# Folding the value norms into the output weights, and four buffers for the copied attention products

## Chip, cores and metric

The kernel runs on one core of one Trainium2 chip. The metric is the device time in microseconds (us) of one execution. One pair of numbers is kept apart throughout: the time of an execution, and the span, which is the stretch from the first to the last instruction that the profiler recorded in it.

## The reference

Four sequences of 512 tokens and width 512 go through one transformer layer: layer norm, attention, layer norm, residual; then layer norm, a gated feed-forward, layer norm, residual. The part that matters here:

```python
xq = rms_norm(x @ wq.T, q_norm_w)      # 32 query heads of 64
xk = rms_norm(x @ wk.T, k_norm_w)      # 8 key heads, each used by 4 query heads
xv = x @ wv.T                          # 8 value heads, each used by 4 query heads
scores = q @ k.T / 8 + alibi           # causal, window of 256 keys
out = softmax(scores) @ v
y = out.reshape(tokens, 2048) @ wo.T   # wo: 512 x 2048
```

Values are float32. The kernel gets float32 accuracy from TensorE by splitting every operand into a rounded part and a remainder (`_hi`, `_lo`) and adding three products.

## The kernel before

**Stage 1, projections.** For each sequence the queries, keys and values are computed and stored to DRAM. The value weights are first divided by a norm for each value column (`vn`, 512 numbers, one for each of 8 x 64 columns), so that values fit a pair of float16 numbers. The norms are computed once into a tile whose 128 partitions all hold the same 512 numbers, and stored to DRAM as `vn_scr` (128 x 512). So the attention's product has to be multiplied by `vn` again somewhere.

**Stage 2, attention and output projection.** Sixteen pairs of value heads are worked through, `for n in range(16)`: pair `n` holds value heads `2n` and `2n + 1` over all sequences (`s` = 0, 1 inside a pair), and for each of them four tiles of 128 queries (`i`), and for each of those four query heads: 32 units `u` in a pair. A unit is: scores (PE, L1322), bias and clamp (DVE `u_sb`, L1030), exponential (ACT `p_sb`, L781), transposes (PE, L1410), rounding and remainder (ACT `pT_hi`, DVE `pT_lo`), products with the values (PE, L1426 to L1428). Every engine runs a fixed order of work; a later step of a unit runs a few units behind the first. From pair 4 on PE also runs the output projection of one tile for each pair (L1449), four pairs behind; in pairs 0 to 3 there is none.

After each four units (one query tile of four heads, numbered `a` = 8n + 4s + i here) the product is finished:

- `take_values` (ACT, L901) copies 4 x 65 columns out of PSUM into `o_raw`; column 64 is the sum of the probabilities. There are two buffers, and the copy `a` waits until `o_mid` of `a - 2` is done.
- `invert_sums` (DVE, L1156) takes the reciprocals into `inv_sum`, also two buffers.
- `finish_o` (POOL) runs two operations: `o_mid = o_raw * inv_sum` (L672), then, after a wait for the first, `o_out = o_mid * v_norm` (L678).
- `store_o` (SP, L474) stores `o_out` to DRAM.

POOL's order in pair `n` is written out by hand:

```python
for i in range(2, 4): finish_o(n - 1, 1, i)
make_bias(n, 1)                 # needed by DVE's unit 16 of pair n
split_late(n, 0, 16)            # two late normalisations' remainders
for i in range(4):
    finish_o(n, 0, i)
    if tile < 0 and i in (2, 3): split_wo(n, i - 2)
make_bias(n + 1, 0)             # needed by DVE's unit 0 of pair n + 1
split_late(n, 16, 32)           # three of them
for i in range(2):
    finish_o(n, 1, i)
    if tile < 0: split_wo(n, 2 + i)
```

`tile = n - 4`, so `split_wo` runs in pairs 0 to 3 only: it makes `wo_hi` and `wo_lo` of one 128 x 512 chunk of the output weights (16 chunks, loaded four at a time by `load_wo` on SP). The late normalisations are those of the last sequence's queries and keys, which stage 1 leaves over: 17 of them in units 2, 4, 18, 20 and 22 of pairs 0 to 3 (five in each of pairs 0 to 2, two in pair 3); each is a DVE operation (`raw`, L1070), an ACT rounding (`qk`, L824), a POOL remainder (`qk`, L697) and a store on SP (L444). After the last one, in pair 3, SP waits until all stores of stage 1 have landed (`stage1_stored`), then stores `o_out`, and then loads keys and queries of pair 4 (`load_heads`, L457 and L458).

**Stage 3, the rest.** Four tiles of the output projection are left at 896 us, and then the feed-forward runs until the end.

Of the kernel before, what the change touches and what calls it, by code (L numbers as in the profile page):

```python
# [25 lines left out]
F32 = mybir.dt.float32  # L26
# [3 lines left out]
ALU = mybir.AluOpType  # L30

P = 128
B, T, D = 4, 512, 512
H, G, HD = 32, 8, 64
REP = H // G
# [3 lines left out]
TT = T // P  # L39
# [31 lines left out]
AHEAD = 2  # L71
TWINS = LAG * UNITS - 2 * TT
RING = 4
PIECE = 3
DMA = 16
RATIO = 2.0 ** (-8.0 / H)
# [2 lines left out]
O_COLS = HD + 1  # L79
# [103 lines left out]
def at_least(eng, sem, value):  # L183

    if isinstance(value, int) and value <= 0:
        return
    eng.wait_ge(sem, value)
# [18 lines left out]
def sandwich_layer(nc, x, wqT, wkT, wvT, woT, q_norm, k_norm, gateT, upT, downT, gate_s, up_s, down_s, out):  # L206
# [9 lines left out]
    vn_scr = nc.dram_tensor("vn_scr", [P, G * HD], F32, kind="Internal").ap()  # L216
    z_scr = nc.dram_tensor("z_scr", [B * TT, P, D], F32, kind="Internal").ap()

    with ExitStack() as ctx:
        def sb(scope, name, shape, dt=F32):  # L220
            return scope.enter_context(nc.sbuf_tensor(name, shape, dt))
# [4 lines left out]
        def sems(names):  # L226
            return [sem(name) for name in names.split()]
# [41 lines left out]
        with ExitStack() as s2:  # L269
            q_st = sb(s2, "q_st", [P, 2, REP, T], F32R)  # L270
            k_st = sb(s2, "k_st", [P, 2, 2, T], F32R)
            v_st = sb(s2, "v_st", [P, 2, TT, V_COLS], F16)
            bias1 = sb(s2, "bias1", [P, REP, WIN])
            y_raw = sb(s2, "y_raw", [P, D])
            sb(s2, "spare4", [P, REP * WIN - D])
            v_norm = sb(s2, "v_norm", [P, G + 2, HD])
            f_bits = sb(s2, "f_bits", [P, PARTS, D])
            used_bits = sb(s2, "used_bits", [P, D])
            u_sb = sb(s2, "u_sb", [P, RING, WIN])
            low = sb(s2, "low", [P, RING])  # L280
            p_sb = sb(s2, "p_sb", [P, RING, WIN])
            pT_hi = sb(s2, "pT_hi", [P, RING, WIN], F16)
            pT_lo = sb(s2, "pT_lo", [P, RING, WIN], F16)
            inv_sum = sb(s2, "inv_sum", [P, 2, REP])
            sb(s2, "spare", [P, REP * HD])
            o_raw = sb(s2, "o_raw", [P, 2, REP, O_COLS])
            o_mid = sb(s2, "o_mid", [P, REP, HD])
            o_out = sb(s2, "o_out", [P, TT, REP, HD])
            wo_stage = sb(s2, "wo_stage", [P, TT, D])
            wo_hi = sb(s2, "wo_hi", [P, QC, D], F32R)  # L290
            wo_lo = sb(s2, "wo_lo", [P, QC, D], F32R)
            o_in = sb(s2, "o_in", [P, 2, TT, 2 * REP * HD])
            oT_hi = sb(s2, "oT_hi", [P, 2, 4, P], F32R)
            oT_lo = sb(s2, "oT_lo", [P, 2, 4, P], F32R)
            x_res = sb(s2, "x_res", [P, D])
            y_n = sb(s2, "y_n", [P, D])
            z_out = sb(s2, "z_out", [P, D])
            sb(s2, "spare3", [P, S1_END - S2_END])
            bias = [sb(s2, "bias0", [P, REP, WIN]), bias1]
# [3 lines left out]
        with ExitStack() as s4:  # L303
# [41 lines left out]
        dist_ready, bias_ready, vn_loaded = sems("dist_ready bias_ready vn_loaded")  # L345
        s_psum, u_ready, p_ready, pT_psum, pT_hi_ready, pT_ready, pv_done = sems(
            "s_psum u_ready p_ready pT_psum pT_hi_ready pT_ready pv_done")
        inv_sum_ready, o_raw_ready, o_mid_ready, o_ready = sems(
            "inv_sum_ready o_raw_ready o_mid_ready o_ready")
        tile_loaded, tile_last = sems("tile_loaded0 tile_loaded1"), sems("tile_last0 tile_last1")  # L350
        wo_hi_ready, wo_ready, res1_loaded, oT_psum, oT_hi_ready, oT_ready, oT_used = sems(
            "wo_hi_ready wo_ready res1_loaded oT_psum oT_hi_ready oT_ready oT_used")
# [32 lines left out]
        def hold(eng):  # L385


            eng.sem_inc(held, 1)
# [3 lines left out]
        def _(sp):  # L392
# [155 lines left out]
                store_o(n, 1, 0)  # L548

            sp.wait_ge(gemm_done, NGEMM * B)  # L550
            sp.dma_start(v_norm[:, 0:G].rearrange("p g d -> p (g d)"), vn_scr).then_inc(vn_loaded, DMA)
            sp.dma_start(v_norm[:, G:G + 2].rearrange("p g d -> p (g d)"), vn_scr[:, 0:2 * HD]).then_inc(vn_loaded, DMA)
            for n in range(B * TT):
                attend(n)
            for i in range(1, TT):
# [65 lines left out]
        def _(pool):  # L621
# [45 lines left out]
            def finish_o(n, s, i):  # L667

                a = 2 * TT * n + TT * s + i
                pool.wait_ge(inv_sum_ready, a + 1)  # L670
                at_least(pool, o_ready, a)
                nc.gpsimd.tensor_tensor(out=o_mid[:], in0=o_raw[:, i % 2, :, 0:HD],  # L672
                                        in1=inv_sum[:, i % 2].unsqueeze(2).broadcast_to([P, REP, HD]),
                                        op=ALU.mult).then_inc(o_mid_ready, 1)
                pool.wait_ge(o_mid_ready, a + 1)
                at_least(pool, o_stored[i], DMA * (2 * n + s))
                hold(pool)
                nc.gpsimd.tensor_tensor(out=o_out[:, i], in0=o_mid[:],  # L678
                                        in1=v_norm[:, 2 * (n % TT) + s:2 * (n % TT) + s + 1].broadcast_to([P, REP, HD]),
                                        op=ALU.mult).then_inc(o_ready, 1)  # L680

            def split_wo(group, i):
                chunk = bass.ds(TT * group + i, 1)
                pool.wait_ge(wo_loaded, DMA * (group + 1))
                hold(pool)
                nc.gpsimd.tensor_copy(wo_hi[:, chunk], wo_stage[:, i:i + 1]).then_inc(wo_hi_ready, 1)
                pool.wait_ge(wo_hi_ready, TT * group + i + 1)
                hold(pool)
                nc.gpsimd.tensor_tensor(out=wo_lo[:, chunk], in0=wo_stage[:, i:i + 1], in1=wo_hi[:, chunk].bitcast(F32),
                                        op=ALU.subtract).then_inc(wo_ready, 1)  # L690

            def split_late(n, first, end):
# [78 lines left out]
        def _(act):  # L771
# [124 lines left out]
            def take_values(n, u):  # L896

                a = 2 * TT * n + u // REP
                act.wait_ge(pv_done, UNITS * n + u + 1)
                at_least(act, o_mid_ready, a - 1)  # L900
                nc.scalar.activation(o_raw[:, u // REP % 2].rearrange("p r d -> p (r d)"),  # L901
                                     bank[4 + u // REP % 2][:, 0:REP * O_COLS], ACT.Copy).then_inc(o_raw_ready, 1)

            def round_oT(t, m, banks=(6,)):
# [82 lines left out]
        def _(dve):  # L987
# [163 lines left out]
            def invert_sums(n, u):  # L1151

                a = 2 * TT * n + u // REP
                dve.wait_ge(o_raw_ready, a + 1)
                at_least(dve, o_mid_ready, a - 1)
                nc.vector.reciprocal(inv_sum[:, u // REP % 2], o_raw[:, u // REP % 2, :, HD]).then_inc(inv_sum_ready, 1)  # L1156

            def split_oT(t, m, banks=(6,)):
                dve.wait_ge(oT_hi_ready, 4 * t + m + 1)
# [449 lines left out]
```

## Time and profile before

| | us |
|---|---|
| median of three runs | 1206.97 (1206.37 to 1208.41) |
| the profiled execution's own time | 1207.18 |
| its span | 1205.0 |
| PE busy | 1164.7 (97%) |
| DVE busy | 891.2 (74%) |
| ACT busy | 745.9 (62%) |
| POOL busy | 392.1 (33%), 465 instructions |

The span is 2.2 us shorter than the execution. Busy times are sums over stages with different limits: in the table PE looks like the limit everywhere, and POOL, with a third of the span, like an engine that can't matter. Stage 1 ends at about 295 us, pairs 0 to 3 run from there to about 428 us, pairs 4 to 15 to 896 us.

### The profile page before, as it was taken

How to read it: one execution, taken by the hardware profiler on the slowest of the kernel's cores; microseconds unless marked ns; L12 is line 12 of the kernel's file. 1: busy time of each engine (PE TensorE's matmuls, PEld its weight loads, DVE VectorE, ACT ScalarE, POOL GpSimd, SP SyncE). 2: the span in 40 equal slices, each digit the busy share in tenths (PEclk: the TensorE clock that was granted, in tenths of full speed). 3: DMA queues.
4: the chain of work that ended last, by engine and by line, in shares of the span. 5: the costliest groups of instructions: out<-in, count | busy, mean ns of one | idle time of the engine just before them, and what ended most of it. 6: DMA issues, size and time to landing. Idle time of an engine off the chain costs nothing.

```text
span 1205.0 us, 26933 instructions
## 1 busy us (share of the span) xinstructions
PE 1164.7 (97%) x9016; PEld 994.3 (83%) x9016; DVE 891.2 (74%) x2328; ACT 745.9 (62%) x1582; POOL 392.1 (33%) x465
## 2 busy tenths in 40 slices
PE   7999999999888899999999999999999999999997
PEld 5878888887777788898989898898888888888876
DVE  5587778687888878888888888888866575546464
ACT  4646555555888778888878888788862443222230
POOL 3000000001799865354544545354531100202022
PEclk9999999999999999999999999999999999999999
DMA  5216355347667774556545664556437440303020
GB/s 175 105 45 245 141 212 206 140 193 261 215 232 246 245 252 137 184 164 220 158 152 178 205 203 139 179 171 217 128 95 237 146 130 30 105 1 106 1 70 36
DMA packets 100132, 189.89 MB, mean 158 GB/s; under 512 B 8352, under 2 KB 38176, under 8 KB 100000
## 3 DMA queue, kind: packets, MB, share of 16 engines
q1 hardware_dynamic: 100000, 188.21, 46.3%
q8 instruction: 73, 1.20, 0.4%
q14 instruction: 59, 0.48, 0.1%
HBM read 116.54 MB, written 71.63 MB: 156 GB/s over the span
## 4 chain that ended last, share of the span: by engine, by line
PE 88%; POOL 5%; DVE 3%; issue 2%; ACT 1%; DMA 1%; SPq 0%; POOLq 0%; DVEq 0%; ACTq 0%
PE bank L1384 21%; PE bank L1517 19%; PE bank L1449 15%; PE bank L1322 11%; PE bank L1410 10%; PE bank L1428 2%; PE bank L1438 2%; PE bank L1426 2%; PE bank L1427 2%; POOL qk L697 1%; POOL bias L663 1%; POOL o_mid L672 1%; DMA q_st<-q_scr 1%; POOL o_out L678 1%; PE bank L1494 1%
## 5 line engine op out<-in xcount | busy, mean ns | idle before, releaser
L781 ACT ACTIVATE p_sb<-u_sb,low 128x384 f32<-128x384 f32 (+2 forms) x512 | 272.5, 536 | 49.4 <-DVE low L1030 40.8
L1030 DVE CUSTOM_DVE_ANT_0 u_sb<-bank,bias 128x384 f32<-128x384 f32 (+2 forms) x512 | 229.8, 452 | 50.8 <-PE bank L1322 28.2
L1322 PE MATMUL bank<-k_st,q_st 128*128 128x384 f32 (+2 forms) x1024 | 254.7, 331 | 1.9 <-DMA q_st<-q_scr 1.4
L1410 PE MATMUL bank<-ident,p_sb 128*128 128x128 f32 x1152 | 218.3, 280 | 21.0 <-ACT p_sb L781 13.7
L1144 DVE TENSOR_TENSOR pT_lo<-bank,pT_hi 128x384 f16<-128x384 f32 (+2 forms) x392 | 178.5, 455 | 34.5 <-ACT pT_hi L889 27.4
L889 ACT ACTIVATE pT_hi<-bank 128x384 f16<-128x384 f32 (+2 forms) x392 | 159.9, 408 | 42.9 <-PE bank L1410 38.3
L1322 PEld LDWEIGHTS bank<-k_st,q_st 128*128 128x128 f32 x1024 | 170.5, 193 | 18.9 <-DMA q_st<-q_scr 1.7
L1410 PEld LDWEIGHTS bank<-ident,p_sb 128*128 128x128 f32 x1152 | 141.1, 141 | 51.3 <-ACT p_sb L781 27.9
L672 POOL TENSOR_TENSOR o_mid<-o_raw,inv_sum 128x256 f32<-128x256 f32 x128 | 83.8, 654 | 227.8 <-DVE inv_sum L1156 226.3
L634 POOL TENSOR_TENSOR rstd<-var_eps,minus_half 128x1 f32<-128x1 f32 (+1 forms) x30 | 22.6, 752 | 413.8 <-DVE var_eps L999 413.8
L1517 PE MATMUL bank<-zT_hi,gu 128*128 128x512 f32 x352 | 139.3, 396 | 0.6 <-DVE hid L1273 0.6
L1517 PE MATMUL bank<-zT_lo,gu 128*128 128x512 f32 x352 | 138.1, 392 | 0.0
L1426 PE MATMUL bank<-v_st,pT_hi 128*128 128x65 f16 x1152 | 131.8, 193 | 0.5 <-DVE pT_lo L1144 0.5
L1427 PE MATMUL bank<-v_st,pT_hi 128*128 128x64 f16 x1152 | 131.8, 193 | 0.0
L1428 PE MATMUL bank<-v_st,pT_lo 128*128 128x65 f16 x1152 | 131.4, 194 | 0.0
L1384 PE MATMUL bank<-xT_hi,w_hi 128*128 128x512 f32 x320 | 127.4, 398 | 0.9 <-DVE xT_lo L1044 0.9
L1384 PE MATMUL bank<-xT_hi,w_lo 128*128 128x512 f32 x320 | 125.1, 391 | 0.0
L1384 PE MATMUL bank<-xT_lo,w_hi 128*128 128x512 f32 x320 | 125.0, 391 | 0.0
L663 POOL TENSOR_TENSOR bias<-dist,slopes 128x1536 f32<-128x1536 f32 x32 | 87.9, 2748 | 106.1 <-DVE low L1030 101.2
L1449 PE MATMUL bank<-wo_hi,oT_hi 128*128 128x512 f32 x256 | 115.4, 451 | 0.8
L1426 PEld LDWEIGHTS bank<-v_st,pT_hi 128*128 128x128 f16 x1152 | 109.0, 99 | 0.7 <-DVE pT_lo L1144 0.6
L1427 PEld LDWEIGHTS bank<-v_st,pT_hi 128*128 128x128 f16 x1152 | 107.0, 97 | 3.0
(128 smaller groups left out, 2396.1 us busy)
## 6 DMA issues: line engine op xcount, KB each, us to landing
q_scr<-qk SPq DMA_DIRECT2D x64, 512.0 KB, 2.7
q_st<-q_scr SPq DMA_DIRECT2D x32, 1024.0 KB, 7.8
k_st<-k_scr SPq DMA_DIRECT2D x64, 256.0 KB, 3.2
o_scr<-o_out SPq DMA_DIRECT2D x128, 128.0 KB, 2.9
o_in<-o_scr SPq DMA_DIRECT2D x16, 768.0 KB, 5.2
k_scr<-qk SPq DMA_DIRECT2D x16, 512.0 KB, 2.6
z_in<-z_scr SPq DMA_DIRECT2D x8, 1024.0 KB, 5.9
v_scr<-v_out SPq DMA_DIRECT2D x4, 1040.0 KB, 6.6
```

What stands on the lines that cost most here:

```text
L781: nc.scalar.activation(p_sb[:, u % RING, 0:w], u_sb[:, u % RING, 0:w], ACT.Exp, scale=-1.0, bias=low[:, u % RING:u % RING + 1]).then_inc(p ...
L889: nc.scalar.activation(pT_hi[:, at, 0:w], bank[probability_bank(A)][:, 0:w], ACT.Copy).then_inc(pT_hi_ready, 1)
L1030: nc.vector.tensor_tensor_reduce(out=u_sb[:, u % RING, 0:w], in0=bank[u % 2][:, 0:w], in1=bias[2 * u // UNITS][:, u % REP, at:at + w], sca ...
L1144: nc.vector.tensor_tensor(pT_lo[:, at, 0:w], bank[probability_bank(A)][:, 0:w], pT_hi[:, at, 0:w], ALU.subtract).then_inc(pT_ready, 1)
L1322: mm = nc.tensor.matmul(bank[u % 2][:, 0:w], q_st[:, s, r, P * i:P * i + P], k_st[:, s, part, P * key:P * key + w], start=(part == 0), sto ...
L1384: mm = nc.tensor.matmul(bank[n % 4][:], lhs, rhs, start=(kc == 0 and k == 0), stop=(kc == KC - 1 and k == 2))
L1410: mm = nc.tensor.transpose(bank[probability_bank(A)][:, P * j:P * j + P], p_sb[:, u % RING, P * j:P * j + P], ident[:])
L1426: nc.tensor.matmul(acc, hi, v_hi, start=(j == 0), stop=False, skip_group_check=True)
L1427: nc.tensor.matmul(acc[:, 0:HD], hi, v_lo, start=False, stop=False, skip_group_check=True)
L1428: mm = nc.tensor.matmul(acc, lo, v_hi, start=False, stop=(j == tiles - 1), skip_group_check=True)
L1449: mm = nc.tensor.matmul(acc[:], lhs, rhs, start=(chunk == 0 and k == 0), stop=(chunk == QC - 1 and k == 2))
L1517: mm = nc.tensor.matmul(acc, lhs, rhs, start=(first and k == 0), stop=(last and k == len(products) - 1))
```

## The change

The norms no longer multiply the attention's product. They are multiplied into the rows of the output weights instead, in `split_wo`, before these are split: one more POOL operation for each of 16 chunks (128 x 512), in place in `wo_stage`. `finish_o` is left with one operation instead of two, 128 times. The norms are loaded for that as a column: `vn_col` has 128 partitions and 8 columns, partition `d` of each half of 64 holding norm `64g + d` in column `g`, read from one row of `vn_scr`, element by element. `o_raw` and `inv_sum` have four buffers, and their writers wait for `o_out` of `a - 4` where they waited for `o_mid` of `a - 2`. The late normalisations stay in the units they were in. Two `hold` calls (a semaphore increment each) go from `split_wo`. The tiles behind `o_raw` move by 64 bytes in each partition.

```diff
+O_RING = TT
@@ buffers
-            v_norm = sb(s2, "v_norm", [P, G + 2, HD])
+            vn_col = sb(s2, "vn_col", [P, G])
+            sb(s2, "spare5", [P, (G + 2) * HD - G])
-            inv_sum = sb(s2, "inv_sum", [P, 2, REP])
-            sb(s2, "spare", [P, REP * HD])
-            o_raw = sb(s2, "o_raw", [P, 2, REP, O_COLS])
-            o_mid = sb(s2, "o_mid", [P, REP, HD])
+            inv_sum = sb(s2, "inv_sum", [P, O_RING, REP])
+            o_raw = sb(s2, "o_raw", [P, O_RING, REP, O_COLS])
@@ SP, before the pairs
-            sp.dma_start(v_norm[:, 0:G].rearrange("p g d -> p (g d)"), vn_scr).then_inc(vn_loaded, DMA)
-            sp.dma_start(v_norm[:, G:G + 2].rearrange("p g d -> p (g d)"), vn_scr[:, 0:2 * HD]).then_inc(vn_loaded, DMA)
+            for half in range(2):
+                sp.dma_start(vn_col[HD * half:HD * half + HD, :], vn_scr[0].rearrange("(g d) -> d g", g=G),
+                             allow_slow_non_contiguous=True).then_inc(vn_loaded, DMA)
@@ POOL, finish_o
                 pool.wait_ge(inv_sum_ready, a + 1)
-                at_least(pool, o_ready, a)
-                nc.gpsimd.tensor_tensor(out=o_mid[:], in0=o_raw[:, i % 2, :, 0:HD],
-                                        in1=inv_sum[:, i % 2].unsqueeze(2).broadcast_to([P, REP, HD]),
-                                        op=ALU.mult).then_inc(o_mid_ready, 1)
-                pool.wait_ge(o_mid_ready, a + 1)
                 at_least(pool, o_stored[i], DMA * (2 * n + s))
                 hold(pool)
-                nc.gpsimd.tensor_tensor(out=o_out[:, i], in0=o_mid[:],
-                                        in1=v_norm[:, 2 * (n % TT) + s:2 * (n % TT) + s + 1].broadcast_to([P, REP, HD]),
+                nc.gpsimd.tensor_tensor(out=o_out[:, i], in0=o_raw[:, i, :, 0:HD],
+                                        in1=inv_sum[:, i].unsqueeze(2).broadcast_to([P, REP, HD]),
                                         op=ALU.mult).then_inc(o_ready, 1)
@@ POOL, split_wo
-                chunk = bass.ds(TT * group + i, 1)
+                chunk = TT * group + i
+                g = 2 * chunk // REP
                 pool.wait_ge(wo_loaded, DMA * (group + 1))
-                hold(pool)
-                nc.gpsimd.tensor_copy(wo_hi[:, chunk], wo_stage[:, i:i + 1]).then_inc(wo_hi_ready, 1)
+                nc.gpsimd.tensor_tensor(out=wo_stage[:, i], in0=wo_stage[:, i], in1=vn_col[:, g:g + 1].broadcast_to([P, D]),
+                                        op=ALU.mult).then_inc(wo_scaled, 1)
+                pool.wait_ge(wo_scaled, chunk + 1)
+                nc.gpsimd.tensor_copy(wo_hi[:, chunk], wo_stage[:, i]).then_inc(wo_hi_ready, 1)
...
@@ ACT take_values and DVE invert_sums
-                at_least(act, o_mid_ready, a - 1)
+                at_least(act, o_ready, a - O_RING + 1)
```

## Rows read from the trace of the kernel before

**Rows 1.** The page, 40 slices of 30.1 us each: PE and POOL, busy tenths

```profile
PE   7999999999888899999999999999999999999997
...
POOL 3000000001799865354544545354531100202022
```

**Rows 2.** Windows: length, then busy us (count) of PE, PEld, DVE, ACT, POOL

```profile
337.60:372.40 34.80, 29.44 (x354) 24.92 (x354) 29.66 (x94) 28.68 (x62) 31.57 (x33) 0.95 0.71 237
436.00:864.00 428.00, 424.06 (x4590) 383.77 (x4590) 359.82 (x1267) 348.85 (x850) 203.84 (x221) 1.00 0.55 177
```

**Rows 3.** Waits from 297 to 436 us: total, times, longest

```profile
ACT o_raw L901 <- POOL o_mid L672: 12.0, 9, 2.9
...
DVE u_sb L1030 <- POOL bias L663: 2.0, 2, 1.0
...
PEld bank L1322 <- DMA q_st<-q_scr: 1.7, 1, 1.7
```

**Rows 4.** Timeline of POOL, 304 to 435 us: start, duration, line, operation, idle before

```profile
304.17 0.61 POOL L672 TENSOR_TENSOR o_mid<-o_raw,inv_sum 128x256 f32<-128x256 f32 x1 [1.34 <-DVE inv_sum L1156]
...
311.79 1.03 POOL L672 TENSOR_TENSOR o_mid<-o_raw,inv_sum 128x256 f32<-128x256 f32 x1 [2.59 <-DVE inv_sum L1156]
...
334.39 0.62 POOL L672 TENSOR_TENSOR o_mid<-o_raw,inv_sum 128x256 f32<-128x256 f32 x1
335.21 0.73 POOL L678 TENSOR_TENSOR o_out<-o_mid,v_norm 128x256 f32<-128x256 f32 x1 [0.20 <-POOL o_mid L672]
336.09 0.61 POOL L672 TENSOR_TENSOR o_mid<-o_raw,inv_sum 128x256 f32<-128x256 f32 x1
...
349.06 0.62 POOL L686 CAST wo_hi<-wo_stage 128x512 fp32r<-128x512 f32 x1
349.86 1.28 POOL L689 TENSOR_TENSOR wo_lo<-wo_stage,wo_hi 128x512 fp32r<-128x512 f32 x1 [0.18 <-POOL wo_hi L686]
...
372.38 2.75 POOL L663 TENSOR_TENSOR bias<-dist,slopes 128x1536 f32<-128x1536 f32 x1
...
407.15 2.75 POOL L663 TENSOR_TENSOR bias<-dist,slopes 128x1536 f32<-128x1536 f32 x1
...
434.77 0.61 POOL L672 TENSOR_TENSOR o_mid<-o_raw,inv_sum 128x256 f32<-128x256 f32 x1 [0.53 <-DVE inv_sum L1156]
```

**Rows 5.** Groups of POOL, shapes apart: busy us, mean ns

```profile
L678 POOL TENSOR_TENSOR o_out<-o_mid,v_norm 128x256 f32<-128x256 f32 x128 | 98.3, 768 | 26.0 <-POOL o_mid L672 23.8 <-DVE low L1030 2.2
L663 POOL TENSOR_TENSOR bias<-dist,slopes 128x1536 f32<-128x1536 f32 x32 | 87.9, 2748 | 106.1 <-DVE low L1030 101.2 <-PE bank L1384 4.9
L672 POOL TENSOR_TENSOR o_mid<-o_raw,inv_sum 128x256 f32<-128x256 f32 x128 | 83.8, 654 | 227.8 <-DVE inv_sum L1156 226.3
...
L755 POOL TENSOR_TENSOR y_s<-y_s,z_in 128x512 f32<-128x512 f32 x15 | 20.6, 1398 | 7.9 <-DVE y_s L1017 5.9 <-DVE y_s L1301 2.0
```

**Rows 6.** Timeline of DVE: unit 0 of pair 2, unit 16 of pair 3, unit 0 of pair 4

```profile
357.59 0.29 DVE L1030 CUSTOM_DVE_ANT_0 u_sb<-bank,bias 128x128 f32<-128x128 f32 x1 [1.00 <-POOL bias L663]
...
410.12 0.29 DVE L1030 CUSTOM_DVE_ANT_0 u_sb<-bank,bias 128x128 f32<-128x128 f32 x1
...
428.22 0.29 DVE L1030 CUSTOM_DVE_ANT_0 u_sb<-bank,bias 128x128 f32<-128x128 f32 x1
```

**Rows 7.** Timeline of SP's queue and of PE: loads of norms and pair 4's queries

```profile
296.43 1.25 SPq L552 DMA_DIRECT2D v_norm<-vn_scr  x1
...
417.91 0.59 SPq L458 DMA_DIRECT2D q_st<-q_scr  x1
...
427.60 0.44 PE L1322 MATMUL bank<-k_st,q_st 128*128 128x128 f32 x2 [1.43 <-DMA q_st<-q_scr]
```

**Rows 8.** DMA issues: count, KB each, median us from issue to landing

```profile
q_st<-q_scr SPq DMA_DIRECT2D x32, 1024.0 KB, 7.8
...
v_norm<-vn_scr SPq DMA_DIRECT2D x1, 256.0 KB, 6.6
...
gate_sc<-gate_s SPq DMA_DIRECT2D x1, 5.5 KB, 7.7
```

More of the change, by code:

```diff
@@ L347, in sandwich_layer @@
             "s_psum u_ready p_ready pT_psum pT_hi_ready pT_ready pv_done")
-        inv_sum_ready, o_raw_ready, o_mid_ready, o_ready = sems(
-            "inv_sum_ready o_raw_ready o_mid_ready o_ready")
+        inv_sum_ready, o_raw_ready, wo_scaled, o_ready = sems(
+            "inv_sum_ready o_raw_ready wo_scaled o_ready")
         tile_loaded, tile_last = sems("tile_loaded0 tile_loaded1"), sems("tile_last0 tile_last1")
@@ L670, in finish_o @@
                 pool.wait_ge(inv_sum_ready, a + 1)
-                at_least(pool, o_ready, a)
-                nc.gpsimd.tensor_tensor(out=o_mid[:], in0=o_raw[:, i % 2, :, 0:HD],
-                                        in1=inv_sum[:, i % 2].unsqueeze(2).broadcast_to([P, REP, HD]),
-                                        op=ALU.mult).then_inc(o_mid_ready, 1)
-                pool.wait_ge(o_mid_ready, a + 1)
                 at_least(pool, o_stored[i], DMA * (2 * n + s))
                 hold(pool)
-                nc.gpsimd.tensor_tensor(out=o_out[:, i], in0=o_mid[:],
-                                        in1=v_norm[:, 2 * (n % TT) + s:2 * (n % TT) + s + 1].broadcast_to([P, REP, HD]),
+                nc.gpsimd.tensor_tensor(out=o_out[:, i], in0=o_raw[:, i, :, 0:HD],
+                                        in1=inv_sum[:, i].unsqueeze(2).broadcast_to([P, REP, HD]),
                                         op=ALU.mult).then_inc(o_ready, 1)
             def split_wo(group, i):
-                chunk = bass.ds(TT * group + i, 1)
+                chunk = TT * group + i
+                g = 2 * chunk // REP
                 pool.wait_ge(wo_loaded, DMA * (group + 1))
-                hold(pool)
-                nc.gpsimd.tensor_copy(wo_hi[:, chunk], wo_stage[:, i:i + 1]).then_inc(wo_hi_ready, 1)
-                pool.wait_ge(wo_hi_ready, TT * group + i + 1)
-                hold(pool)
-                nc.gpsimd.tensor_tensor(out=wo_lo[:, chunk], in0=wo_stage[:, i:i + 1], in1=wo_hi[:, chunk].bitcast(F32),
+                nc.gpsimd.tensor_tensor(out=wo_stage[:, i], in0=wo_stage[:, i], in1=vn_col[:, g:g + 1].broadcast_to([P, D]),
+                                        op=ALU.mult).then_inc(wo_scaled, 1)
+                pool.wait_ge(wo_scaled, chunk + 1)
+                nc.gpsimd.tensor_copy(wo_hi[:, chunk], wo_stage[:, i]).then_inc(wo_hi_ready, 1)
+                pool.wait_ge(wo_hi_ready, chunk + 1)
+                nc.gpsimd.tensor_tensor(out=wo_lo[:, chunk], in0=wo_stage[:, i], in1=wo_hi[:, chunk].bitcast(F32),
                                         op=ALU.subtract).then_inc(wo_ready, 1)
@@ L899, in take_values @@
                 act.wait_ge(pv_done, UNITS * n + u + 1)
-                at_least(act, o_mid_ready, a - 1)
-                nc.scalar.activation(o_raw[:, u // REP % 2].rearrange("p r d -> p (r d)"),
+                at_least(act, o_ready, a - O_RING + 1)
+                nc.scalar.activation(o_raw[:, u // REP % O_RING].rearrange("p r d -> p (r d)"),
                                      bank[4 + u // REP % 2][:, 0:REP * O_COLS], ACT.Copy).then_inc(o_raw_ready, 1)
@@ L1154, in invert_sums @@
                 dve.wait_ge(o_raw_ready, a + 1)
-                at_least(dve, o_mid_ready, a - 1)
-                nc.vector.reciprocal(inv_sum[:, u // REP % 2], o_raw[:, u // REP % 2, :, HD]).then_inc(inv_sum_ready, 1)
+                at_least(dve, o_ready, a - O_RING + 1)
+                nc.vector.reciprocal(inv_sum[:, u // REP % O_RING], o_raw[:, u // REP % O_RING, :, HD]).then_inc(inv_sum_ready, 1)
             def split_oT(t, m, banks=(6,)):
```

## Prediction

> **What bounds the kernel now.** I read the slices first, because the change touches POOL, and POOL is busy for only a third of the span. The reader is to see that this third is uneven: POOL shows 7 to 9 tenths in six slices after 300 us, in just the slices where PE falls to 8 tenths [rows 1]. The second view is the windows of those stretches. From 436 to 864 us PE is busy 424.06 of 428.00 us [rows 2]: there PE is the bound, and no work taken from POOL, ACT or DVE can shorten it. From 337.60 to 372.40, one whole pair, PE is busy 29.44 of 34.80 us, DVE 29.66, ACT 28.68 and POOL 31.57 [rows 2]. No engine is full by this count, so the third view is the waits. ACT waits 12.0 us for `o_mid` in nine pieces, DVE 2.0 us for a bias and PE's loads 1.7 us for the queries of pair 4 [rows 3]. The first two are waits for POOL. The fourth view, POOL's own timeline, settles it: POOL last waits for data at 311.79 (2.59 us) and next at 434.77 (0.53 us) [rows 4]; between these its only gaps are those of 0.2 us and less ahead of an operation that reads the one before. The bias for the second half of a pair starts at 372.38 and at 407.15 [rows 4], 34.77 us apart, and that is the pace of the pairs. So POOL, with these gaps, bounds pairs 0 to 3 from 312 us to about 412 us, and nothing later.
>
> What the other engines would allow is well below that pace. In one pair, 372.38 to 407.15, the wait for POOL on DVE is 1.0 us [rows 6], and ACT's share of its 12.0 us is about 4; 34.8 less 5 is some 30 us, near PE's 29.44.
>
> **What the change takes from POOL in that stretch.** Before, one finish followed by another takes 336.09 - 334.39 = 1.70 us: `o_mid` starts, 0.82 us later `o_out`, which lasts 0.73, then 0.15 until the next starts [rows 4]. After it is one operation with the operands of `o_mid` (0.61) and the gap of 0.15: 0.76. It saves 0.94. If the one operation took as long as `o_out` does (0.73), it would save 0.82; that is the dear bound. I take 0.94, since the inputs and their strides are those of `o_mid` and only the place written differs.
>
> Per chunk of `wo` one multiply is added, with a wait for it before the rounding. The trace has no such operation. Two rows have its form of a second input that is one number per partition repeated along the columns: `o_mid`, 256 columns, 0.61, and the bias, 1536 columns, 2.748 [rows 4, 5]. A line through them gives 0.61 + 256 x (2.748 - 0.61) / 1280 = 1.04 us for 512 columns. The wait behind it is 0.2, as before `o_out` [rows 4]: 1.24 for each chunk. Bounds: cheap, a rounding with one input, 0.62 + 0.20 = 0.82 [rows 4]; dear, `y_s`, an operation in place on 512 columns with two full inputs, 1.398 + 0.20 = 1.60 [rows 5]. I take 1.24, because the two rows on the line share its form. The two `hold` calls that go are worth at most a part of these small gaps, and count as nothing; that they are on POOL's busy stretch could only add to the gain.
>
> The Trainium skill (GPSIMD Engine Reference, Elementwise, side-by-side cycle accounting) gives about 2.6 cycles of a 1.2 GHz clock for each element of an operation with two inputs. By it the multiply would take about 1.11 us without its start, an estimate from that page. The remainder of `wo` with 512 columns and two inputs at 1.28 us [rows 4] fits it; the bias, at 1.79 ns for each column, is below its 2.17 ns, so for the repeated form the rows decide. With the page's figure the gain below would be 0.8 us smaller.
>
> **The sum.** The stretch that POOL sets runs from 311.79 to the bias of pair 3's second half at 407.15. By POOL's written order it holds `finish_o` 2 and 3, 4 to 7, and all eight of pairs 1 and 2: 22 of them. It holds four chunks of `wo` in each of pairs 0, 1 and 2: 12. So that bias starts 22 x 0.94 - 12 x 1.24 = 20.7 - 14.9 = 5.8 us earlier, at 401.35.
>
> Does PE follow in full? With two buffers ACT was held when POOL was one or two finishes late; with four it may be nearly twice as far ahead, and I expect its 12.0 us of waits to go. But the bias stays: DVE can't start unit 16 of a pair before POOL has worked through that queue, and a pair now costs POOL 34.77 - 8 x 0.94 + 4 x 1.24 = 32.2 us, still over the 30 that the others need. So the stall isn't removed, it is moved from ACT's copy to DVE's unit 16 (and a little at unit 0), some 2 us in each of pairs 1 to 3, and only POOL's net relief is gained: 2.6 us for a pair. Before, unit 16 of pair 3 ran at 410.12 [rows 6], 0.2 us after its bias was done (407.15 + 2.75); after, at about 404.1.
>
> From there to pair 4, at 428.22, it is 18.1 us [rows 6], and the last thing that ends is the load of the queries: issued at 417.91, waited for until 427.60 [rows 7]. It is queued on SP behind the last late normalisations' stores, which follow POOL's remainders after that same bias. So it moves by the same 5.8 us, and so does pair 4. If the load lands in its median of 7.8 us [rows 8] and not in 9.7 as here, the wait of 1.43 goes too, and the gain is 7.2.
>
> After pair 4 PE is the bound, idle for 3.94 us in 428 [rows 2], so the shift passes to the end. There 96 more finishes lose an operation and save nothing. The larger product: 1207.18 - 5.8 = 1201.4 for the profiled execution. Its time is 0.2 above the median of the runs, so I forecast 1201.2.
>
> **Edits that cost nothing.** The norms are loaded in 1,024 pieces of 4 bytes. The first `finish_o` waits for them; it starts at 304.17, after 1.34 us of waiting for data, and the next idle stretches of POOL are over 2 us each, to 311.79 [rows 4]. The loads before were issued by 296.43 and took 6.6 us [rows 7, 8]. So a landing up to about 310 is hidden by POOL's idle time and by ACT's four buffers. The smallest load in the trace, 5.5 KB in short rows, takes 7.7 us [rows 8], which would mean 304. Queued behind the norms on SP is the first load of `wo`, which isn't read before 312.8. The shift of 64 bytes changes no operation. `wo_stage` is in use for longer by the multiplies, but its next load is queued on SP behind the stores of two later finishes, so it doesn't wait for them.
>
> **Rivals.** *The multiply is dear.* If it costs 1.60 and a finish saves 0.94, the gain is 20.7 - 19.2 = 1.5, time 1205.5; at 1.28 + 0.20 it is 2.9, time 1204.1. For it speaks that it writes in place as `y_s` does; against it the line through the two rows of its own form. *The stall only moves.* With a finish that saves 0.82 and a multiply at 1.48, 18.0 - 17.8 = 0.2: 1206.8, no change, although ACT's 12.0 us are gone from the waits. *The buffers free everything.* If POOL were no longer needed in time, all of the 12.0 + 2.0 would go and 1193 be reached. Against it: 32.2 us of POOL work for a pair of 30. A cheap multiply of 0.82 would give 20.7 - 9.8 = 10.9, near it, 1196.1.
>
> *Slower: the column load holds POOL.* `finish_o` 0 can't start until both loads land, and the whole queue stands behind it. Up to about 310 nothing is lost; every us beyond delays the stretch by one. At a landing of 316, twenty us after the issue, the 5.8 us are used up, and beyond it the kernel is slower: 25 us would give 1212. The nearest rows, 6.6, 7.7 and 7.8 us [rows 8], speak against it, though none has pieces of 4 bytes.
> The Trainium skill (DMA: Bandwidth & Descriptors, Rules for kernel authors) speaks against this load: a last dimension that isn't contiguous becomes one descriptor for each element, and a transpose by a rearranged pattern is 19 times slower than its own transpose. No row here shows such a load. By that factor on 6.6 us the norms would land after 125 us and the time be some 110 us longer, an estimate from that page; I hold it unlikely for two loads of 2 KB.
>
> **Chances and range.** POOL's net relief between 4.4 and 7.4 us, the forecast: 0.60. A dearer multiply with 2.4 to 4.4 left: 0.16. More than 7.4 (cheap multiply, or more freed): 0.08. Stall only moves, within 2.4 either way: 0.11. Slower by the load: 0.05. What a measurement can tell from no change is about 0.2%, 2.4 us. So faster 0.84, same 0.11, slower 0.05. The range of 8 in 10 leaves out the slow case and the ends of the multiply's bounds: 1198.6 to 1204.8.
>
> **What the profile after would show.** ACT's waits for POOL before `o_raw` near zero between 297 and 436 us. DVE's waits for the bias up from 2.0 to some 5 or 7 us, in pieces of 1 to 2.5. The multiply at about 1.04 us and `o_out` at 0.61. Biases of a pair's second half 32.2 us apart, the one of pair 3 near 401.4. POOL busy down by 128 x 0.768 and up by 16 x 1.04, from 392 to about 310, with 353 instructions. PE's busy time unchanged. Pair 4 near 422.4, and the same difference at every later point. I am wrong if ACT still waits for POOL (the buffers weren't the coupling), if the biases come closer than 31 us without DVE waiting (POOL wasn't the pace), if `finish_o` 0 starts after 310, or if something between pair 4 and the end gives the gain back.

## The result, and the profile after

The changed kernel takes 1198.89 us (median of four, 1198.33 to 1198.96), beside 1207.69 for the kernel before in the same runs: a ratio of 0.9927, 95% interval 0.9915 to 0.994, or 8.8 us. Timed once more beside the experiments it was 1198.82 against 1207.23, 0.9928 (0.9914 to 0.9942). The forecast was 5.8 us less than before, 1201.2, with a range of 1198.6 to 1204.8. The span of the profiled execution fell from 1205.0 to 1197.1 us.

The page after, in 40 slices of 29.9 us each, against [rows 1]:

```profile
PE   7999999999989899999999999999999999999997
...
POOL 3000000000799933323232323233211100202022
```

POOL is down to 2 or 3 tenths after pair 3, but in pairs 0 to 3 it is as full as it was. Over the span it is busy 308.6 us with 353 instructions (forecast: about 310), and PE 1162.5 where it was 1164.7 and had been forecast unchanged. The windows, against [rows 2]; the second one starts 8 us earlier than there:

```profile
337.60:372.40 34.80, 31.32 (x395) 26.61 (x392) 31.97 (x104) 31.41 (x68) 32.96 (x30) 1.00 0.76 254
428.00:856.00 428.00, 424.31 (x4590) 384.31 (x4589) 360.85 (x1272) 349.14 (x852) 134.34 (x133) 1.00 0.57 178
```

The same 34.8 us now hold 395 matmuls where they held 354. The waits between 297 and 436 us, against [rows 3]:

```profile
POOL o_out L674 <- DVE inv_sum L1155: 15.4, 9, 3.5
...
PE bank L1437 <- DMA o_in<-o_scr: 2.3, 1, 2.3
...
DVE u_sb L1029 <- POOL bias L664: 1.5, 3, 0.5
```

ACT's 12.0 us are gone, and DVE's waits for the bias are 1.5 us where I had written some 5 to 7. A wait of PE for a load of `o_in` is new. POOL's timeline, against [rows 4]:

```profile
312.79 0.93 POOL L674 TENSOR_TENSOR o_out<-o_raw,inv_sum 128x256 f32<-128x256 f32 x1 [3.50 <-DVE inv_sum L1155]
...
359.83 1.48 POOL L683 TENSOR_TENSOR wo_stage<-wo_stage,vn_col 128x512 f32<-128x512 f32 x1
...
363.88 1.04 POOL L683 TENSOR_TENSOR wo_stage<-wo_stage,vn_col 128x512 f32<-128x512 f32 x1
364.98 0.61 POOL L686 CAST wo_hi<-wo_stage 128x512 fp32r<-128x512 f32 x1
365.67 1.29 POOL L688 TENSOR_TENSOR wo_lo<-wo_stage,wo_hi 128x512 fp32r<-128x512 f32 x1
366.91 1.19 POOL L674 TENSOR_TENSOR o_out<-o_raw,inv_sum 128x256 f32<-128x256 f32 x2
368.06 2.75 POOL L664 TENSOR_TENSOR bias<-dist,slopes 128x1536 f32<-128x1536 f32 x1
...
375.73 0.91 POOL L674 TENSOR_TENSOR o_out<-o_raw,inv_sum 128x256 f32<-128x256 f32 x1 [0.67 <-DVE inv_sum L1155]
...
399.53 2.74 POOL L664 TENSOR_TENSOR bias<-dist,slopes 128x1536 f32<-128x1536 f32 x1
```

One chunk is 366.91 - 363.88 = 3.03 us; before it was 351.10 (the next `o_mid`) less 349.06, 2.04 [rows 4]. Two finishes take 1.15 us together, and the biases of a pair's second half are 399.53 - 368.06 = 31.47 apart, where they were 34.77. In pairs 1 and 2 POOL waits for data once each, 0.67 us. The groups, against [rows 5]:

```profile
L674 POOL TENSOR_TENSOR o_out<-o_raw,inv_sum 128x256 f32<-128x256 f32 x128 | 81.1, 635 | 319.5 <-DVE inv_sum L1155 319.5
...
L683 POOL TENSOR_TENSOR wo_stage<-wo_stage,vn_col 128x512 f32<-128x512 f32 x16 | 18.0, 1124 | 0.0
```

For the way through the stage I take the start of DVE's reciprocal (`inv_sum`) of the finish `a` in each profile, and count from that of `a` = 0. That takes out a difference which isn't the change's: the stage began at 304.75 in the first profile of the changed kernel, at 303.21 in the second, and at 303.85 before. Finish 28 lies in the second half of pair 3, 32 is the first of pair 4, and 124 lies in the second half of pair 15. The kernels marked e1 to e9 are those of the experiments below.

| us after finish 0 | 16 | 28 | 32 | 124 |
|---|---|---|---|---|
| before | 68.03 | 118.50 | 135.62 | 581.64 |
| changed kernel | 62.32 | 109.22 | 128.16 | 573.20 |
| changed kernel, second profile | 62.33 | 109.22 | 127.18 | 572.33 |
| e1, buffers only | 65.29 | 116.54 | 135.57 | 580.69 |
| e2, fold only | 66.46 | 115.15 | 131.93 | 577.44 |
| e3, no multiply | 62.19 | 108.76 | 124.92 | 569.95 |
| e4, holds back | 63.17 | 110.80 | 128.62 | 573.78 |
| e5, wait later (second profile) | 62.32 | 109.22 | 125.14 | 570.31 |
| e6, bias first | 65.28 | 113.68 | 132.19 | 577.27 |
| e7, three buffers | 62.31 | 109.43 | 126.66 | 572.21 |
| e8, multiply twice | 69.58 | 124.58 | 140.50 | 585.56 |
| e9, bias and load first | 62.33 | 109.23 | 125.16 | 570.22 |

So the gain is 9.3 us at finish 28, 7.5 (second profile 8.4) at finish 32, and 8.4 (9.3) at finish 124. Three things are to be explained: why 9.3 and not 5.8, what takes back 0.9 to 1.8 before pair 4, and what adds 0.9 afterwards. A part of the 9.3 lies in the marker itself. From POOL's bias for the second half of pair 3 to finish 28 it takes 15.2 us before, 14.4 in the changed kernel and 14.0 with the buffers alone (e1): where ACT is held for POOL, the reciprocal behind its copy comes late as well. Up to that bias the gain is 8.5 us.

**The granted clock of TensorE** is a rival that the prediction doesn't name. The window from 337.60 to 372.40 has a granted clock of 0.95 before [rows 2] and of 1.00 in the changed kernel. Before, the clock was at the lower of its two levels (1.2 of 2.4 GHz) for 3.4 us twice between 304 us and pair 4, from 364.3 and from 398.4, each time shortly (1.2 and 0.5 us) after PE had stood idle for 2.65 us behind ACT, which POOL held. The changed kernel has no such stretch there; in its first profile it has one from 417.2, 0.9 us after PE's wait of 2.34 us for `o_in`, and in its second profile none. The end of PE's first idle stretch before and the window behind it, and the window in the changed kernel:

```profile
363.10 0.33 PE L1410 MATMUL bank<-ident,p_sb 128*128 128x128 f32 x1 [2.65 <-ACT p_sb L781]
...
364.30:367.70 3.40, 2.95 (x18) 2.34 (x17) 1.87 (x8) 2.44 (x7) 3.10 (x4) 0.50 0.76 231
```

```profile
417.30:420.60 3.30, 3.30 (x28) 3.14 (x27) 2.49 (x7) 2.64 (x6) 2.42 (x3) 0.51 1.03 365
```

Up to the last bias that DVE waits for, the clock doesn't explain the gain: before, POOL waits for no data from 311.79 to 434.77 [rows 4], so a slower PE holds nothing there, and e2 takes 33.22 us for its first eight finishes without such a stretch and 33.24 and 33.23 for the next two eights with one in each. Behind finish 28, where POOL no longer sets the pace, it can count: the second profile, without the stretch, is 1.0 us ahead at finish 32. No run separates that from the different waits of the two.

### The profile page after: what moved, and what is told of

It is laid out like the page before. It is cut to its first block, busy times and chain, and to the rows that moved or that the text cites. A ratio compares the mean times of both kernels' runs of the same rounds, so it can differ in the third digit from the quotient of the medians.

```text
span 1197.1 us, 26657 instructions
## 1 busy us (share of the span) xinstructions
PE 1162.5 (97%) x9016; PEld 993.8 (83%) x9016; DVE 889.9 (74%) x2328; ACT 745.1 (62%) x1582; POOL 308.6 (26%) x353
## 4 chain that ended last, share of the span: by engine, by line
PE 86%; POOL 6%; DVE 3%; issue 2%; ACT 1%; DMA 1%; SPq 0%; POOLq 0%; DVEq 0%; ACTq 0%
PE bank L1383 21%; PE bank L1516 19%; PE bank L1448 15%; PE bank L1321 10%; PE bank L1409 9%; PE bank L1437 2%; PE bank L1427 2%; PE bank L1425 2%; PE bank L1426 2%; POOL bias L664 1%; POOL qk L696 1%; POOL wo_stage L683 1%; POOL o_out L674 1%; POOL wo_hi L686 1%; PE bank L1493 1%
## 5 line engine op out<-in xcount | busy, mean ns | idle before, releaser
L674 POOL TENSOR_TENSOR o_out<-o_raw,inv_sum 128x256 f32<-128x256 f32 x128 | 81.1, 635 | 319.5 <-DVE inv_sum L1155 319.5
L635 POOL TENSOR_TENSOR rstd<-var_eps,minus_half 128x1 f32<-128x1 f32 (+1 forms) x30 | 22.6, 752 | 423.1 <-DVE var_eps L998 423.1
```

## The experiments

All kernels were timed in five rounds beside the kernel before. The first four shared a chip, e5 to e8 another, and e9, e5 once more and the changed kernel once more a third. The ratios are taken over all runs, so they aren't quite the quotients of the two medians.

**e1: the buffers alone.**

```diff
-            inv_sum = sb(s2, "inv_sum", [P, 2, REP])
-            o_raw = sb(s2, "o_raw", [P, 2, REP, O_COLS])
+            inv_sum = sb(s2, "inv_sum", [P, O_RING, REP])      # O_RING = 4
+            o_raw = sb(s2, "o_raw", [P, O_RING, REP, O_COLS])
-                at_least(act, o_mid_ready, a - 1)
+                at_least(act, o_mid_ready, a - O_RING + 1)
```

> The kernel before with one part of the change: four buffers of o_raw and inv_sum, and their writers wait for o_mid of a - 4. finish_o keeps its two operations and split_wo its two. Nothing of the computation is left out. Theory A (POOL's work sets the pace of pairs 0 to 3, the buffers only move where the stall shows): ACT's 12.0 us of waits for o_mid go nearly to zero, DVE's waits for the bias rise from 2.0 to over 8 us, the biases stay 34.8 us apart, and the time is within 1.5 us of before, 1206 to 1208. Rival B (the two buffers were the coupling that cost the time): 1200 to 1202 and biases closer than 33 us.

1206.47 us against 1206.92, ratio 0.9989 (0.9979 to 1.0). The waits of that kernel from 297 to 436 us:

```profile
DVE u_sb L1030 <- POOL bias L663: 7.6, 5, 2.2
POOL o_mid L672 <- DVE inv_sum L1156: 7.6, 4, 2.6
...
PE bank L1322 <- DMA q_st<-q_scr: 2.3, 1, 2.3
```

and two biases of its POOL:

```profile
372.52 2.75 POOL L663 TENSOR_TENSOR bias<-dist,slopes 128x1536 f32<-128x1536 f32 x1
...
407.10 2.75 POOL L663 TENSOR_TENSOR bias<-dist,slopes 128x1536 f32<-128x1536 f32 x1
```

ACT doesn't wait for POOL any more, DVE waits 7.6 us instead of 2.0, and the pace is 34.58 us for a pair. With the buffers alone the 12.0 us of waits that the view of before shows on ACT are worth 0.5 us by the medians (1.3 by the ratio, whose interval reaches up to no gain): the stall changes its place. That is theory A, though with 7.6 us of waits on DVE where it had over 8, and it is the prediction's rival "the stall only moves", made real by leaving out the fold. In the table e1 is 2.0 us ahead at finish 28 and 0.1 at finish 32: PE waits 2.3 us for the queries, where it was 1.4 before, in the queue that e5 is about.

**e2: the fold alone.**

```diff
-O_RING = TT
+O_RING = 2
-                nc.gpsimd.tensor_tensor(out=o_out[:, i], in0=o_raw[:, i, :, 0:HD],
+                nc.gpsimd.tensor_tensor(out=o_out[:, i], in0=o_raw[:, i % O_RING, :, 0:HD],
```

> The changed kernel with two buffers of o_raw and inv_sum in use, and the writers waiting for o_out of a - 2; norms folded into the weights, one operation in finish_o. Nothing of the computation is left out. Theory A: POOL's relief of 8 to 9 us up to pair 3 is gained here too; ACT's waits come back in part (4 to 8 us) in place of DVE's for the bias; time 1199 to 1201.5. Rival B (the buffers are the larger part): 1204 to 1207.

1204.18 us against 1206.92, 0.9973 (0.9963 to 0.9984): 2.7 us (3.3 by the ratio). The time lies just inside rival B's 1204 to 1207, but its reason fails, since e1 shows the buffers alone to be the smaller part; ACT's waits are those of theory A, its time isn't. Both of my theories were too simple here. Its waits and its timeline in pair 1:

```profile
POOL o_out L674 <- DVE inv_sum L1155: 18.6, 8, 3.5
...
ACT o_raw L900 <- POOL o_out L674: 7.1, 5, 2.0
```

```profile
341.05 1.19 POOL L674 TENSOR_TENSOR o_out<-o_raw,inv_sum 128x256 f32<-128x256 f32 x2
345.24 0.91 POOL L674 TENSOR_TENSOR o_out<-o_raw,inv_sum 128x256 f32<-128x256 f32 x1 [3.00 <-DVE inv_sum L1155]
```

While POOL makes a bias and three late remainders, 7.1 us in one piece, two buffers fill and ACT stands for 1.97 us. In the half before, and again in the next pair, POOL has caught up and stands itself, for 3.00 us, because the finish that it wants comes from a pipeline that was held. The relief of POOL is there, but it is spent as idle time of POOL. So the two parts need each other: 0.5 us for the buffers, 2.7 for the fold, 8.4 to 8.8 for both (by the ratios 1.3, 3.3 and 8.7 to 8.8).

**e3: without the multiply.**

```diff
-                nc.gpsimd.tensor_tensor(out=wo_stage[:, i], in0=wo_stage[:, i], in1=vn_col[:, g:g + 1].broadcast_to([P, D]),
-                                        op=ALU.mult).then_inc(wo_scaled, 1)
-                pool.wait_ge(wo_scaled, chunk + 1)
```

> The changed kernel without the multiply of the norms into the weights, so the value norms are left out of the computation; split_wo rounds the weights as loaded. It prices the added operation where it stands. The multiply lasts 1.04 us and up to 1.48, and the rounding starts 0.07 later, some 1.15 for a chunk; 12 of them before the last bias that DVE waits for are 13.8 us of POOL. Theory A in full (POOL still the pace): another 8 us or more, 1190. Theory C (with the multiply POOL is only just the pace, the other engines come next at about 31 us for a pair): DVE's waits for the bias of 1.5 us go and little more, 1196.5 to 1198.5, with POOL waiting for data for over 8 us more between 312 and 420.

1195.49 us against 1206.92, 0.9907 (0.9892 to 0.9921), between the two expectations and nearer to theory C. Of POOL's window of 34.8 us only 26.07 are busy:

```profile
337.60:372.40 34.80, 31.49 (x403) 26.62 (x401) 32.05 (x104) 31.52 (x69) 26.07 (x24) 1.00 0.83 289
```

POOL has over 8 us to spare, and still finish 28 comes only 0.5 us earlier than in the changed kernel. From finish 16 to 24, one pair, it takes 396.28 - 365.18 = 31.10 us: that is what the other engines need, not the 30 that I had worked out. The 2.6 to 3.0 us in time come behind finish 28, probably because the last late stores leave POOL earlier and with them the queue that e5 is about; no run separates this.

**e4: the holds put back.**

```diff
+                hold(pool)
                 nc.gpsimd.tensor_copy(wo_hi[:, chunk], wo_stage[:, i]).then_inc(wo_hi_ready, 1)
                 pool.wait_ge(wo_hi_ready, chunk + 1)
+                hold(pool)
```

> The changed kernel with the two semaphore increments (hold) put back in split_wo, ahead of the rounding and ahead of the remainder. Nothing of the computation is left out. My sum counted them as nothing, yet the stretch of POOL became 3 us shorter than it said, and the gap between rounding and remainder is 0.08 us where it was 0.18. If the increment sits in the dependent gap: gaps back to 0.2, 24 x 0.11 = 2.6 us more of POOL up to pair 3, and 1 to 2.6 us in time, 1200 to 1201.5. If the gap comes from elsewhere: the same time as the changed kernel within 0.5, 1198.4 to 1199.4.

1198.55 us against 1206.92, 0.9939 (0.9924 to 0.9954). Its POOL in pair 1:

```profile
348.12 1.04 POOL L683 TENSOR_TENSOR wo_stage<-wo_stage,vn_col 128x512 f32<-128x512 f32 x1
349.33 0.61 POOL L687 CAST wo_hi<-wo_stage 128x512 fp32r<-128x512 f32 x1 [0.17 <-POOL wo_stage L683]
350.12 1.28 POOL L690 TENSOR_TENSOR wo_lo<-wo_stage,wo_hi 128x512 fp32r<-128x512 f32 x1 [0.18 <-POOL wo_hi L687]
351.37 2.74 POOL L664 TENSOR_TENSOR bias<-dist,slopes 128x1536 f32<-128x1536 f32 x1
```

The gaps are back, and a chunk is 351.37 - 348.12 = 3.25 us, 0.22 more than without. That is the price of the increments when they stand between an operation and the one that waits for it. In the way through the stage it shows: finish 28 comes 1.6 us later. By finish 32 only 0.5 to 1.4 of it is left, and the time doesn't resolve it: the median is that of the changed kernel, the ratio 1.4 us above it, and the two intervals overlap.

**e5: SP's wait for stage 1 moved.**

```diff
             def attend(n):
+                if n == 2 * LAG:
+                    stage1_stored(B)
...
                 for f in late_norms(n, first, end):
                     store_qk(B - 1, f)
-                    if f == QC + KVC - 1:
-                        stage1_stored(B)
```

> The changed kernel with SP's wait for all stores of stage 1 (stage1_stored) moved from after the last late normalisation of pair 3 to the start of pair 8; only pairs 12 to 15 read what it guards. Nothing of the computation is left out. In the changed kernel PE waited 2.3 us in pair 3 for o_in, whose load is queued behind this wait, and 1.8 us of what had been gained by the middle of pair 3 was given back by pair 4. If that queue gave it back: no wait of PE for o_in or q_st in pair 3 or 4, and 1.5 to 2.5 us faster than the changed kernel, 1196.4 to 1197.4. If something else holds pair 4 (POOL's bias of the next pair, PE itself): 1198.5 to 1199.

> e5_wait_later once more, beside the kernel before, the changed kernel and e9 on one chip, for their differences. Theory: 2 to 3 us faster than the changed kernel, 1195.5 to 1196.5.

1195.89 us against 1207.91 (0.9895, 0.9881 to 0.991), and 1196.41 against 1207.23 (0.9906, 0.9891 to 0.9921), where the changed kernel was 1198.82 on the same chip: 2.4 us less. There the two intervals just overlap, but the slowest of four runs of e5 (1196.95) is below the fastest of five of the changed kernel (1196.97), and the first measurement of e5 agrees. The queue of SP in the changed kernel, and behind it the row of PE that waits (both timelines):

```profile
403.53 1.76 SPq L444 DMA_DIRECT2D k_scr<-qk  x2
409.23 0.33 SPq L474 DMA_DIRECT2D o_scr<-o_out  x1
409.67 1.48 SPq L484 DMA_DIRECT2D o_in<-o_scr  x1
```

```profile
416.28 0.63 PE L1437 MATMUL bank<-ident,o_in 128*128 128x128 f32 x4 [2.34 <-DMA o_in<-o_scr]
```

and the queue of SP in e5 (second profile):

```profile
403.67 1.76 SPq L444 DMA_DIRECT2D k_scr<-qk  x2
405.67 0.33 SPq L474 DMA_DIRECT2D o_scr<-o_out  x1
406.11 1.28 SPq L484 DMA_DIRECT2D o_in<-o_scr  x1
```

The reader is to see the 3.9 us between the end of the `k_scr` stores' row and the next store of `o_scr`; in e5 they are 0.2. SP's own waits in the changed kernel, from 397 to 430 us, name the landing of the keys:

```profile
SPq L449 <- DMA k_scr<-qk: 3.7, 1, 3.7
```

In its second profile this wait is 4.0 us, before it was 2.7. What it guards is read by pairs 12 to 15 only. Before the change, when POOL held everything back, PE missed the load of `o_in` by 0.6 us and that of the queries by 1.4 [rows 7]. With the pairs 9 us ahead, the units of pair 3 reach both loads sooner: the changed kernel's first profile shows `o_in` missed by 2.34 us, its second `o_in` by 0.7 and the queries by 2.2. In e5 only the queries are missed, by 0.2 and 0.7, and the clock is at its upper level from 304 us to pair 4 in both profiles; whatever the lower level costs the changed kernel there is part of the 2.4 us. Finish 32 comes 2.0 to 3.0 us earlier in e5, while 16 and 28 are at the same place.

**e6 and e9: the bias ahead of the leftover finishes.**

```diff
+                    if tile < 0:
+                        make_bias(n, 1)
                     for i in range(TT // 2, TT):
                         finish_o(n - 1, 1, i)
...
-                    make_bias(n, 1)
+                    if tile >= 0:
+                        make_bias(n, 1)
```

> As e5_wait_later, and in pairs 1 to 3 POOL makes the bias of the pair's second half before the two finishes left over from the pair before instead of after them. Nothing of the computation is left out. DVE waited 0.5 us in each of pairs 1 to 3 for that bias in the changed kernel. If POOL's order is what still costs there: these waits go and 1 to 1.5 us more than e5, 1195 to 1196.4. If POOL's sum of work is the pace and not its order: the wait shows up elsewhere (at the bias of unit 0, or in ACT before o_raw), same time as e5 within 0.5.

1203.93 us against 1207.91, 0.9966 (0.9953 to 0.9979): 8 us slower than e5, which neither expectation had. POOL in pair 1:

```profile
344.41 0.91 POOL L674 TENSOR_TENSOR o_out<-o_raw,inv_sum 128x256 f32<-128x256 f32 x1 [0.67 <-DVE inv_sum L1158]
348.66 1.04 POOL L683 TENSOR_TENSOR wo_stage<-wo_stage,vn_col 128x512 f32<-128x512 f32 x1 [3.34 <-DMA wo_stage<-woT]
```

The finishes that were moved back by one bias are what SP stores next, and the load of the next four chunks of `wo` is queued behind these stores. POOL waits for it 8.9 us in three pieces. e9 moves that load ahead of two of the stores:

```diff
                     store_o(n - 1, 1, 1)
+                if tile < 0:
+                    load_wo(n)
+                if n:
                     store_o(n - 1, 1, 2)
```

> As e6_bias_first, and SP issues the load of the next four chunks of wo right after the store of tile 1, ahead of the stores of tiles 2 and 3 and of load_values. Nothing of the computation is left out. e6 was 8 us slower than e5, with POOL waiting 8.9 us in three pieces for wo_stage: its load is queued on SP behind the store of the finish that the bias now goes ahead of. If that queue is the whole loss: these waits are under 0.5 us each, and the time is that of e5 or up to 1.5 us less, 1194.4 to 1196.2. If making the bias early costs in itself (late finishes hold ACT, late stores hold the ring of qk): it stays over 1198.

1195.45 us against 1207.23, 0.9901 (0.9883 to 0.992). POOL doesn't wait for `wo_stage` any more, so the queue was the whole loss. Against e5 on the same chip (1196.41) the intervals overlap, and in the table the two go together to 0.1 us at every finish, though in e9 DVE waits for no bias at all. Finish 16 to 24 takes 397.30 - 365.86 = 31.44 us in e9 and 398.52 - 367.07 = 31.45 in the changed kernel. So the 1.5 us of DVE's waits that the changed kernel shows were worth nothing: at this pace POOL and the chain of the other engines are level.

**e7: three buffers.** The changed kernel with `a % 3` for the buffer and the waits for `o_out` of `a - 3`.

> The changed kernel with three buffers of o_raw and inv_sum in use instead of four, the writers waiting for o_out of a - 3. Nothing of the computation is left out. By the two traces the longest hold of ACT came in POOL's run of a bias and three late remainders, 7.2 us, a little under two finishes; a third buffer covers it. Theory: no wait of ACT for POOL, same time as with four, 1198.3 to 1199.5. If the fourth buffer is needed: waits of ACT before o_raw return and 1200 to 1203.

1198.33 us against 1207.91, 0.9923 (0.991 to 0.9935), with no wait of ACT for POOL. The time shows nothing of the fourth buffer.

**e8: the multiply twice.**

```diff
+                nc.gpsimd.tensor_tensor(out=spare5[:, 0:D], in0=wo_stage[:, i], in1=vn_col[:, g:g + 1].broadcast_to([P, D]),
+                                        op=ALU.mult).then_inc(wo_scaled, 1)
```

> The changed kernel with the new multiply doubled: after the one in place, a second with the same inputs writes to a spare tile that nothing reads, and the rounding waits for it. It tries the prediction's rival of a dear multiply, at 2.2 us for a chunk. POOL gets 4 x 1.1 us more for each of pairs 0 to 3. If POOL is the pace: biases 35 us or more apart, DVE's waits for them 10 us and more, 11 us lost, 1208 to 1212, no better than the kernel before. If the four buffers absorb it: under 1203.

1211.08 us against 1207.91, 1.0027 (1.0016 to 1.0038): slower than before. The biases of pair 2 and pair 3 start at 376.32 and 412.40, 36.1 us apart, and DVE waits:

```profile
DVE u_sb L1032 <- POOL bias L664: 9.8, 5, 2.8
```

By the ratios it is 12 us slower than the changed kernel, for about 13 us more of POOL up to the last such bias. On this side of the knee (the point where POOL and the other engines take equally long for a pair) POOL's work counts nearly one for one; on the other (e3) 14 us less of it bring 3. The change as made sits at the knee.

**The changed kernel again.**

> The changed kernel once more, on the same chip as e5_again and e9. Theory: 8.5 to 9 us faster than before, 1198.3 to 1199.3. Its profile also tells whether the 0.8 us that it lost to the kernel before in the first matmuls, at 13 to 60 us, belong to it or to the execution.

1198.82 us, as told above. PE's first block of 192 matmuls takes 45.17 us in this profile, 46.10 in the first one of the changed kernel and 45.35 before, and the stage starts 1.54 us earlier than in the first. So the 0.8 us at the start belong to the execution.

## Why the prediction was right, and where its size was off

**The number, and its luck.** The time lies in the range, 0.3 us above its lower end. POOL's net relief of 8.6 us and the gain of 8.8 don't lie in the band of 4.4 to 7.4 that was the forecast (0.60), but in that of more than 7.4, which had 0.08. The mechanism was right; POOL's net relief was put too small by 2.8 us, since two terms were off in the same direction (the finishes by 1.9, the chunks by 2.3, and 1.4 the other way), and what the loads took back before pair 4 brought the result nearer to the forecast.

**POOL sets the pace of pairs 0 to 3, and nothing later.** Right. e1 (waits gone, pace 34.6, time 0.5 us less) and e8 (12 us for 13) show it from both sides. That ACT's large entry in the waits was no gain in itself was the main reading of the prediction, and held. A slip in its first view changes nothing: [rows 1] has four slices of 7 to 9 tenths on POOL, 301 to 422 us, and not six; they are the four in which PE falls to 8.

**Both parts together.** The sum gave the whole gain to POOL's relief and treated the buffers as a place for the stall. That was wrong as a picture of the fold alone: without more buffers POOL idles 3 us in a pair and 2.7 us are left (e2).

**A finish saves 0.94 us.** Measured: before, about 1.49 us to the next start where a chunk or a bias follows and 1.70 where a finish does; after, 0.57 before a chunk (363.31 to 363.88) and 1.15 for two. More is saved where a late normalisation on DVE stretches POOL's operations: the first two finishes of pair 1 take 4.28 us before and 1.63 after. All 22 rows, waits for data left out, come to 37.1 us before and 14.5 after: 22.6, against 20.7.

**A chunk costs 1.24 us more.** This is the term that was mis-sized. The multiply itself was right: 1.04 us, as the line through the two rows of its form had it (1.48 where it meets DVE's late normalisation). But the wait behind it is 0.06, not 0.20, and the gap between rounding and remainder fell from 0.18 to 0.08. A chunk is 0.99 longer (3.03 against 2.04); over the rows of all twelve it is 38.8 us against 26.2, 12.6 more where the sum had 14.9. The sentence that failed is that the two `hold` calls "count as nothing": e4 gives them 0.22 us for a chunk.

**The sum.** 22.6 - 12.6 = 10.0 us, less 1.3 of waiting for data in pairs 1 and 2 and 0.1 in the biases and late remainders, is 8.6; POOL's stretch went from 407.15 - 311.79 = 95.36 to 399.53 - 312.79 = 86.74, 8.6 us, where the prediction had 5.8.

**The others need 30 us for a pair.** They need about 31.1 (e3, where POOL has 8 us to spare). The expected 2 us of DVE's waits in each pair shrank to 0.5, since POOL came down to 31.47 and not 32.2.

**Pair 4 moves by as much.** Not in full: of 9.3 us at finish 28, 7.5 to 8.4 are left at finish 32. I had named the load of the queries and SP's queue, and took it to move with POOL. But `stage1_stored` is a wait for a landing, 3.7 to 4.0 us in the queue where it had been 2.7, and e5 shows that removing it brings 2.4 us. The load of `o_in` in the same queue, which the prediction never priced, was the one missed in the first profile. The clock, which the prediction never priced either, may add to it in that profile.

**After pair 4 the shift passes unchanged.** Nearly: finish 32 to 124 takes 446.02 us before and 445.03 to 445.15 after, about 0.08 us less for each of some twelve pairs. The buffers seem to be enough for it: all kernels with four of them have 445.0 to 445.2, e1 without the fold too; the two that have the fold and fewer, e2 with two buffers and e7 with three, have 445.5. Each figure but that of the changed kernel and e5 is from one profile, and why it is so is open.

**The column load.** Harmless, as forecast: both issued by 298.7, landed 6.2 us after the issue in the median, and the first finish started 0.3 us after its reciprocal.

```profile
vn_col<-vn_scr SPq DMA_DIRECT2D x2, 2.0 KB, 6.2
```

The Trainium skill (DMA: Bandwidth & Descriptors, Rules for kernel authors) states that such a pattern becomes a descriptor for each element; no view here counts the descriptors. With 512 elements a load, 6.2 us is no more than the 6.0 and 6.6 us of the two loads that these replace, and the delay by a factor of 19 did not come. Its figure for operations with two inputs (GPSIMD Engine Reference, Elementwise, side-by-side cycle accounting) overstates the multiply, by 0.07 us even without its start: an estimate of 1.11 against 1.04 measured.

**What beats both kernels.** e5, the changed kernel with one wait moved: 1195.9 and 1196.4 us, 0.9895 and 0.9906 of the kernel before. e9 can't be told from it.

## What to carry to other kernels

A wait in the profile names the place where a bound shows, not what it is worth: buffers on the waiting side and less work on the bounding side gave 0.5 and 2.7 us alone and over 8 together, because POOL works in bursts that two buffers don't cover. When a stretch moves earlier, look down the in-order queue that feeds the next one for a wait that belongs to something read much later; here it cost little before, and it took a part of the gain back. On an engine that never idles, count the gaps between dependent operations as part of their price, and count what is put between them. A forecast of time is checked term by term: here the total came within its range while two of its terms were off the same way.

## What was not expected of the hardware

On POOL a semaphore increment put between an operation and one that waits for its result costs about 0.1 us each: gaps of 0.17 and 0.18 us with it (e4), 0.06 to 0.08 without. In pairs 0 to 3 the multiply took 1.03 to 1.05 us thirteen times and 1.48 to 1.49 three times, each of these while DVE ran a late normalisation, an operation with SBUF inputs only; POOL's roundings and finishes that meet one of these show 0.85 to 1.08 us instead of 0.61. The Trainium skill (SBUF — State Buffer, Who interferes with whom) states that a DVE operation with two SBUF inputs and a GpSimd operation that reads SBUF exclude each other; the durations agree with it, though no run here took the normalisations away.
